# Another order of work in a fused hyena, attention and feed-forward layer: the turn of a batch, the last batch and attention's first tiles

## What is computed

```
x = layernorm(x + hyena(x))        # in-projection to 3 x 256, depthwise conv of 3 taps,
                                   # twice: v = irfft(rfft(v) * rfft(h[n])) * x[n], out-projection
x = layernorm(x + cross_attention(x, ctx))   # 16 heads of 16, 64 context rows per batch
x = layernorm(x + down(silu(gate(x)) * up(x)))  # inner 1024, ternary weights, 8 bit inputs
```

## Time and profile before

| | |
|---|---|
| median of 3 runs | 682.93 us (682.9 to 683.15) |
| profiled execution | 682.95 us, its span 681.0 us |
| TensorE busy | 650.6 us, 96% |
| VectorE busy | 611.0 us, 90% |
| ScalarE busy | 384.5 us, 56% |
| GpSimd busy | 365.1 us, 54% |
| mean granted TensorE clock | 0.998 |

### The profile page before, as it was taken

One profiled execution on the slowest core, in us unless ns is written; L12 is line 12 of the kernel. 1 busy time (PEld: TensorE's weight loads), 2 busy tenths in 40 slices (PEclk: granted clock), 3 DMA queues, 4 the chain that ended last, 5 costly groups with the idle time before them and its releaser, 6 DMA issues. The chain is left out here.

```text
span 681.0 us, 12462 instructions
## 1 busy us (share of the span) xinstructions
PE 650.6 (96%) x4284; PEld 476.8 (70%) x4284; DVE 611.0 (90%) x1241; ACT 384.5 (56%) x761; POOL 365.1 (54%) x506
## 2 busy tenths in 40 slices
PE   9999999999999999999999999888999999999996
PEld 3588765788747887568887677556777775666664
DVE  4899887999999999999999979748999979999997
ACT  3742157131368503475222634569888886888885
POOL 0633424537235753258451381284577769788786
PEclk9999999999999999999999999999999999999999
DMA  8730055230453446443743057552222221010012
GB/s 310 204 63 1 0 125 105 81 62 7 66 107 69 93 155 62 93 93 63 200 100 87 1 185 98 213 174 80 64 80 79 79 79 33 1 34 32 32 63 94
DMA packets 52680, 60.73 MB, mean 89 GB/s; under 512 B 5416, under 2 KB 46376, under 8 KB 52362
## 3 DMA queue, kind: packets, MB, share of 16 engines
q1 hardware_dynamic: 43498, 40.28, 18.3%
q0 software_dynamic: 8256, 18.86, 16.7%
q10 hardware_dynamic: 864, 0.79, 0.4%
HBM read 33.72 MB, written 11.53 MB: 66 GB/s over the span
## 5 line engine op out<-in xcount | busy, mean ns | idle before, releaser
L747 ACT ACTIVATE yb<-banks 128x256 f32<-128x256 f32 x64 | 24.1, 385 | 137.5 <-PE banks L446 92.3
L437 PE MATMUL banks<-inv_m,spec_y 128*128 128x256 f32 x384 | 85.5, 379 | 0.0
L473 PE MATMUL banks<-xt_in,w_in 128*128 128x512 f32 x192 | 84.5, 594 | 0.2
L437 PEld LDWEIGHTS banks<-inv_m,spec_y 128*128 128x128 f32 x384 | 73.0, 190 | 9.9
L389 PE MATMUL banks<-z_cplx,fwd_m 128*128 128x256 f32 x240 | 71.9, 381 | 3.5 <-DVE prod L1172 3.2
L390 PE MATMUL banks<-z_cplx,fwd_m 128*128 128x256 f32 x240 | 71.4, 379 | 0.0
L473 PEld LDWEIGHTS banks<-xt_in,w_in 128*128 128x128 f32 x192 | 36.1, 190 | 43.0 <-issue 40.2
L389 PEld LDWEIGHTS banks<-z_cplx,fwd_m 128*128 128x128 f32 x240 | 44.9, 190 | 11.8 <-issue 5.2
L390 PEld LDWEIGHTS banks<-z_cplx,fwd_m 128*128 128x128 f32 x240 | 45.6, 190 | 6.2
L904 POOL TENSOR_TENSOR spec_y<-prod 128x256 f32<-128x256 f32 x35 | 25.4, 726 | 42.0 <-DVE prod L1172 41.2
L2203 DVE TENSOR_REDUCE peak<-ps_score 128x16 f32<-128x1024 f32 x32 | 38.9, 1215 | 8.7 <-PE ps_score L1668 8.7
(11 more groups left out here) (311 smaller groups left out, 1704.4 us busy)
## 6 DMA issues: line engine op xcount, KB each, us to landing
x_tok<-in_x SPq DMA_DIRECT2D x8, 512.0 KB, 4.3
x_tok<-in_b_out POOLq DMA_DIRECT2D x8, 512.0 KB, 13.9
inv_scratch<-inv_sum SPq DMA_DIRECT2D x16, 256.0 KB, 2.6
xa_t<-inv_scratch SPq DMA_DIRECT2D x16, 256.0 KB, 2.7
v_t<-left POOLq DMA_DIRECT2D x8, 511.5 KB, 5.2
x_t<-left POOLq DMA_DIRECT2D x8, 511.5 KB, 5.6
xt_in<-in_x_t SPq DMA_DIRECT2D x3, 1024.0 KB, 5.9
x_scratch<-x_tok SPq DMA_DIRECT2D x6, 512.0 KB, 4.1
```

The costliest lines, as they stand in the source:

```text
L437: last = mm(bank[:, odd * 2 * P:(odd + 1) * 2 * P], spec_y[:, j + odd, part * D + h * P:part * D + (h + 1) * P], inv_m[:, o:o + 2 * P], st ...
L473: last = mm(proj_pair(b, t)[:, c * 512:(c + 1) * 512], w_in[:, k, TILES[t] * P:(TILES[t] + 1) * P], xt_in[:, k, c * 512:(c + 1) * 512], st ...
```

## The change

Seven edits of order; no arithmetic is added. (1) At the turn of a batch the real pair of `level_one(u + 2, 0)` runs inside `level_two(u + 1, 0)`, and the rotations of the complex pairs run in the next batch, behind the right tap. For that `level_two` keeps its differences in y2 in place of ef. (2) In the last batch `add_residual` is split around `level_two(u, 1)`. (3) There GpSimd makes group 0's factors, four product sums, group 1's factors, and the other sums. (4) ScalarE makes the squares of the last batch's group 0 at the end of `hyena`; `norm_last(0)` no longer waits, and the variance buffer is shared. (5) TensorE's and (6) ScalarE's order of the first six tiles is written out anew, with queries by halves. (7) VectorE's first inverse moves from behind shift 3 to ahead of shift 5.

```diff
@@ hyena, scalar: batch loop's end
             evac_queries(4, IB[0:2])
+            squares(B - 1, (0,))
@@ hyena, gpsimd: batch
                 if last_one:
-                    norm_factors(b - 1)
-                add_products(u + 1)
+                    norm_factors(b - 1, (0,))
+                    add_products(u + 1, 0, 4)
+                    norm_factors(b - 1, (1,))
+                    add_products(u + 1, 4)
+                else:
+                    add_products(u + 1)
@@ hyena, vector: level_two
                 dve.wait_ge(vec_seq, seq.now())
-                signal(tt(ef[:, 0, :], tmp[:, 1, 0:Q], tmp[:, 1, Q:2 * Q], ALU.subtract))
-                signal(tt(ef[:, 1, :], tmp[:, 1, 0:Q], tmp[:, 1, Q:2 * Q], ALU.add))
+                if between is not None:
+                    between()
+                signal(tt(y2[:, 0:Q], tmp[:, 1, 0:Q], tmp[:, 1, Q:2 * Q], ALU.subtract))
+                signal(tt(y2[:, Q:2 * Q], tmp[:, 1, 0:Q], tmp[:, 1, Q:2 * Q], ALU.add))
@@ hyena, vector: batch
                     if not last_one:
                         right_tap(b + 1, T_LEAD)
+                    dve.wait_ge(vec_seq, seq.now())
+                    rotations(in_prod)
                     level_two(u, 0, tmp=past_xq, at=in_prod, u_real=u)
                     level_one(u, 1)
                     dve.wait_ge(vec_seq, seq.now())
                     rotations()
+                    if last_one:
+                        add_residual(b - 1, (0,))
...
                     level_two(u, 1, x0_t[:, 1, :], x0_t[:, 1, :], past_xq, u_real=u)
                     if last_one:
-                        add_residual(b - 1)
+                        add_residual(b - 1, (1,))
...
-                    level_two(u + 1, 0, tmp=past_xq, at=in_prod, u_real=u + 2)
-                    level_one(u + 2, 0, in_prod)
-                    dve.wait_ge(vec_seq, seq.now())
-                    rotations(in_prod)
+                    level_two(u + 1, 0, tmp=past_xq, at=in_prod, u_real=u + 2,
+                              between=lambda: level_one(u + 2, 0, in_prod, complexes=False))
+                    level_one(u + 2, 0, in_prod, real=False)
                     dve.wait_ge(*convolved(b, T_X1 + 1))
                     level_two(u + 1, 1, gate1[:, 1, :], v_t[:, 1, :], past_xq, u_real=u + 2)
@@ attention, tensor (query_half is one of the two bank halves of queries)
             turn_x(Q_EARLY)
-            queries(Q_EARLY)
-            for j in range(TILES_ALL):
+            query_half(Q_EARLY, 0)
+            scores(1)
+            query_half(Q_EARLY, 1)
+            turn_prob(0)
+            turn_x(Q_EARLY + 1)
+            scores(2)
+            turn_prob(1)
+            query_half(Q_EARLY + 1, 0)
+            scores(3)
+            query_half(Q_EARLY + 1, 1)
+            turn_prob(2)
+            turn_x(Q_EARLY + 2)
+            scores(4)
+            turn_prob(3)
+            query_half(Q_EARLY + 2, 0)
+            scores(5)
+            query_half(Q_EARLY + 2, 1)
+            sums(0)
+            scores(6)
+            turn_prob(4)
+            values(0)
+            sums(1)
+            values(1)
+            turn_prob(5)
+            for j in range(6, TILES_ALL):
...
@@ attention, scalar
+            squares_last(0, 2)
             evac_x(Q_EARLY)
-            squares_last(0)
-            for j in range(TILES_ALL):
+            squares_last(2, CH)
+            exponentials(0)
+            act.wait_ge(v_ready, 2 * B)
+            evac_q(Q_EARLY)
+            evac_prob(0)
+            exponentials(1)
+            evac_x(Q_EARLY + 1)
+            evac_prob(1)
+            exponentials(2)
+            evac_q(Q_EARLY + 1)
+            exponentials(3)
+            evac_prob(2)
+            evac_x(Q_EARLY + 2)
+            evac_prob(3)
+            exponentials(4)
+            evac_q(Q_EARLY + 2)
+            weight_sum(0, 0)
+            evac_prob(4)
+            evac_context(0)
+            for j in range(5, TILES_ALL):
...
@@ attention, gpsimd: norm_last
-                pool.wait_ge(l_squared, CH * (g + 1))
+                if g:
+                    pool.wait_ge(l_squared, CH)
@@ attention, vector
+                if j == 5:
+                    invert(0)
                 shift(j)
...
-                if j % 2 and 3 <= j < TILES_ALL - 1:
+                if j % 2 and 5 <= j < TILES_ALL - 1:
                     invert((j - 3) // 2)
```

More of the change, by code:

```diff
@@ L134, in now, with hyena @@
         return self.k
-def hyena(nc, d, x1_dram, fwd_m, w_in, ident, xt_in, x1_even, left, x_toks, row_sum, ld_kv):
+def hyena(nc, d, x1_dram, fwd_m, w_in, ident, xt_in, x1_even, left, x_toks, row_sum, row_var, ld_kv):
     with ExitStack() as ctx:
@@ L763, in row_sums, with squares @@
                     fn(yc[:, 1, :], x_toks[:, g, t, :], ACT.Copy, accum_out=row_sum[:, g, t:t + 1]).then_inc(act_seq, 1)
-            def squares(b):
+            def squares(b, groups=range(GROUPS)):
                 act.wait_ge(first_level, 8 * min(2 * b + 3, 2 * B))
@@ L770, in squares @@
                     act.wait_ge(act_seq, GROUPS * G_OUT * (b + 1) + 1)
-                for g in range(GROUPS):
+                for g in groups:
                     for t in range(G_OUT):
@@ L896, in add_left, with add_products @@
                     .then_inc(conv_done[slot(b, t)], 16)
-            def add_products(u, first=False, prod=prod):
-                for j in range(BANKS - 1):
+            def add_products(u, j0=0, j1=BANKS - 1, first=False, prod=prod):
+                for j in range(j0, j1):
                     pool.wait_ge(prod_done, 8 * u + j + 1)
@@ L951, in add_residual, with norm_factors @@
                     .then_inc(resid_added, 16)
-            def norm_factors(b):
+            def norm_factors(b, groups=range(GROUPS)):
                 ts, tt = nc.gpsimd.tensor_scalar, nc.gpsimd.tensor_tensor
-                for g in range(GROUPS):
+                for g in groups:
                     i = GROUPS * b + g
@@ L1193, in rotations, with level_one @@
                         signal(stt(im, y, -TAN_8, x, ALU.mult, ALU.add))
-            def level_one(u, h, at=None, rotated=False):
+            def level_one(u, h, at=None, rotated=False, real=True, complexes=True):
                 i = 2 * u + h
@@ L1203, in level_one @@
                 split_c = lambda n: yc[:, n, :].rearrange("p (c n) -> p c n", c=2)
-                dve.wait_ge(i_evac, 4 * i + 1)
-                signal(tt(ef[:, 0, :], IB[I_0][:, 0:Q], yb[:, I_0, :], ALU.add))
-                tt(ef[:, 1, :], IB[I_0][:, 0:Q], yb[:, I_0, :], ALU.subtract).then_inc(first_level, 1)
+                if real:
+                    dve.wait_ge(i_evac, 4 * i + 1)
+                    signal(tt(ef[:, 0, :], IB[I_0][:, 0:Q], yb[:, I_0, :], ALU.add))
+                    tt(ef[:, 1, :], IB[I_0][:, 0:Q], yb[:, I_0, :], ALU.subtract).then_inc(first_level, 1)
+                if not complexes:
+                    return
                 for g, bank, factor in ((0, I_2, ROOT_HALF), (1, I_1, COS_8), (2, I_5, COS_8)):
@@ L1214, in level_one, with level_two @@
                         rotations(at, (g,))
-            def level_two(u, h, gate=None, dst=None, tmp=prod, at=None, u_real=None):
+            def level_two(u, h, gate=None, dst=None, tmp=prod, at=None, u_real=None, between=None):
                 i = 2 * u + h
@@ L1275, in quarters_out, with add_residual @@
                 level_two(u, h, gate, dst)
-            def add_residual(b):
-                for g in range(GROUPS):
+            def add_residual(b, groups=range(GROUPS)):
+                for g in groups:
                     dve.wait_ge(biased[g], 16 * (b + 1))
@@ L1464, in attention_loads, with attention_and_feed_forward @@
     return loads
-def attention_and_feed_forward(nc, d, x1_dram, area, small, ident, q_early, x_last, x_last_sum, ld_kv, out):
+def attention_and_feed_forward(nc, d, x1_dram, area, small, ident, q_early, x_last, x_last_sum, l_var, ld_kv, out):
     with ExitStack() as ctx:
@@ L1643, in turn_x, with query_half @@
                     last.then_inc(tr_x, 1)
[L1645 to L1652, removed]
+            def query_half(c, i):
+                if i == 0:
+                    pe.wait_ge(xt_evac, DT * (c - Q_EARLY + 1))
+                t = late_order(c)[i]
+                for k in range(DT):
+                    last = mm(late_banks[t][:, :], wq[:, k, t * P:(t + 1) * P], x_t[:, c % 2, k, :],
+                              start=(k == 0), stop=(k == DT - 1))
+                last.then_inc(q_mm, 1)
             def scores(j):
@@ L1785, in _ @@
                 turn_prob(j)
[L1786 to L1790, removed]
+                if j % 2 == 0:
                     sums(j // 2 - 1)
[L1792 to L1795, removed]
+                    values(j // 2 - 1)
                 if j % 2 and 7 <= j < TILES_ALL - 1:
@@ L1832, in _, with squares_last @@
             fn(table_of[:, 0:1], x_last_sum[:, 0, 0:1], ACT.Exp, scale=0.0)
```

(14 more changed lines are left out.)

9 lines of the change are left out of this document (3 added, 6 removed).

## The result

The changed kernel takes 686.72 us (median of 4 runs, 686.55 to 687.26), the one before 683.04 (4 runs, 682.9 to 683.18): ratio 1.0056, 95% interval 1.0044 to 1.0068. It is slower by 3.7 us. The forecast was 683.4 us, with a range of 680.6 to 685.5. The profiled execution took 686.55, its span is 684.8 us (681.0 before).

A forecast was written before the change was run, and what follows sets the result against it. VectorE was taken to set the pace from batch to batch, with idle time in the last batch and early attention. Terms 0.78 - 1.32 + 1.0 = +0.46 us gave 683.4 us, range 680.6 to 685.5.

The forecast's parts named there:

- Part 1: Turn of a batch, three times: GpSimd's product delays VectorE, 0.26 us each, +0.78 us in all.
- The wait at 263.9: TensorE's 1.11 us wait for VectorE at a batch's turn: would go, its bank coming some 1.1 us sooner.
- the hold: Gated second level: VectorE's first addition held by GpSimd's gating product, 0.26 us a turn, lasting 0.9 instead of 0.69.
- The wait near 290: TensorE's 0.93 us wait for VectorE's right tap: would become about 2 us.
- Part 2: Last batch: earlier GpSimd sums save 1.1 us and additions filling a gap 0.22, -1.32 us in all.
- Part 3: Attention's first tiles: fuller order -0.6 us, GpSimd's holds on VectorE +1.6, together +1.0 us.
- The holds: Attention: GpSimd's scalings and bias addition delay VectorE's paired values and keys; first sum +1.6 us, bounds 0 and 3.4.
- the replay: Attention's new order replayed with the old rows' spacing: without contention the first sum ends as today, order worth -0.6 us.
- the wait of 0.56: Attention, behind the first inverse: VectorE's 0.56 us wait for scores would go.
- B: Attention: stalls of values and keys pass fully to the first sum, 3.4 instead of 1.6; +2.3, 685.2 us; chance 0.19.
- A: VectorE and GpSimd don't hold each other, or keys slip past the bias addition: -1.9, 681.0 us; chance 0.27.
- C: Last batch: VectorE's products 6 and 7 wait for GpSimd sums, the 1.1 is lost: +1.6, 684.5 us; chance 0.06.

The follow-up runs named there:

- the turns alone: The kernel before with only the new turn of a batch, edit (1): 684.57 us, ratio 1.0022.
- attention mended: The kernel before with attention's new order, the first inverse behind shift 5 and the paired keys ahead of GpSimd's bias addition: 679.98 us, ratio 0.9959.
- With the stop filled: The changed kernel with 24 unread identity turns on TensorE between the first sum and scores 6: 686.41 us, ratio 1.0050.
- with the inverse behind shift 5: The changed kernel with only the first inverse moved back behind shift 5 in VectorE's queue: 682.61 us, ratio 0.9994.
- the rows early: The changed kernel with the load of chunk 4's rows issued right behind group 0's reload: 686.61 us, ratio 1.0055.
- all three: The changed kernel with the first inverse behind shift 5, keys ahead of the bias addition and chunk 4's rows loaded early: 679.15 us, ratio 0.9943.
- attention alone: The kernel before with only attention's new order, edits (4) to (7): 686.4 us, ratio 1.0048.

## Why the prediction was wrong

**Part 1, +0.78: right.** 0.77 in the trace of the turns alone, 0.64 at the queries of the changed kernel. The wait at 263.9 is gone and the hold is where it was put. The wait near 290 is not 2 but 0.33 + 1.21, in two places. The Trainium skill, "SBUF — State Buffer", section "Who interferes with whom", says that a VectorE instruction with two SBUF inputs contends with a GpSimd instruction that reads SBUF. The traces agree: the addition took 0.95 us beside GpSimd's product and 0.69 without, and the keys, the pair that no row of the first trace had, took 2.99 us beside the bias addition and 1.02 without.

**Part 2, -1.32: the gain right, the cover wrong.** -1.24 from the queries to the inverse transform. What failed is "From there to the end of the stage TensorE has no gap, so the 1.1 is kept". I followed group 1 to one customer, the bias DMA, and found 3 us of cover. The load of chunk 4's rows stands behind that group's store and reload in SyncE's queue, and it was not in my list. Its cover looked ample: the rows used to land at about 407.5 and are wanted at 415.67, so the 2.06 us of later issue alone would have cost nothing. That the load would take 11.2 us to land in place of 5.0 was in no row, and its cause stays open; issued at 397.20 it took 4.8. Together the two gave back 1.46. Group 1's factors came when I expected them, about 399.

**Part 3, +1.0: the failed step, 2.5 us short.** Measured is +1.93 to the first inverse and +1.60 to the second, and nothing of it comes back behind. The sign of being right that I had named, the second inverse within 1.5 us of its old distance from the barrier, failed with 3.5. The holds were sized nearly right: 1.22 for the keys is shown, and attention mended, which has the keys first, still has its first inverse 0.69 us later behind the barrier than the kernel before; together 1.91, forecast 1.6. The stop was in the replay too: shift 5 until 459.6, and scores 6 behind it, which leaves TensorE idle for 3.4 us from 456.2. What failed is the sentence "The inverse follows at the same time as today; only the wait of 0.56 for scores behind it goes". It gave the steps behind the stop the spacing of rows in which the granted clock was 1.00. They ran in part at 0.50, and the distance of the two inverses became 8.62 in place of 7.02. With the stop filled it is 7.04, so the replay of the order was right and the 1.58 us are the clock, which was in no term of the sum and no rival: I never asked what a stop of TensorE would do to it. The 0.56 did not go either. It comes back before shift 8 (475.57), since ScalarE's copy of tile 4 waits until 466.24 for values 0 and ScalarE works without a gap from there:
```profile
466.24 1.02 ACT L1897 ACTIVATE prob_t<-ps_pt 128x1024 f32<-128x1024 f32 x1 [7.12 <-PE ps_ctx L1716]
```
```profile
475.57 1.23 DVE L2236 TENSOR_REDUCE peak<-ps_score 128x16 f32<-128x1024 f32 x1 [0.56 <-PE ps_score L1680]
```
So part 3 is short by 0.3 (holds), 1.6 (clock) and 0.6 (the wait that stayed), and part 2 by 1.5. By this sum either the clock or the rows alone would have left the time within the range; the two together put it outside. What the replay also missed is no part of the error but the larger lesson: with the inverse behind shift 5 the second inverse follows 3.7 us behind the first, not 7.

**The rivals.** B named keys and values as the slow side and a size of 3.4. The time lies on its side, but not for its reason: TensorE waited 1.16 us before scores 3, not over 2, and the keys' 1.2 is a third of the loss. A did not happen: the keys took 2.99 us, not 1.02. The sign of C did appear: product 6 waited 1.54 us for a GpSimd sum, above the mark of 1 us:
```profile
400.57 0.69 DVE L1175 TENSOR_TENSOR prod<-banks,spec_h 128x512 f32<-128x512 f32 x1 [1.54 <-POOL spec_y L905]
```
But TensorE ran on without a gap into the inverse transform (399.80), so the gain was not lost there, and the mark was not a good one.

## What to carry to other kernels

When an instruction that waits for another engine is moved ahead of one that is ready, the price is the wait of whoever needs the second one: replay both queues, write down the idle time of the engine that sets the pace, and replay the other order too before choosing. When a transfer gets late, list every transfer behind it in its issuing queue, and don't take its landing time from the old trace: here 5.0 us became 11.2. And before a gain is called lost, look at the clock behind the nearest stop of TensorE: two real gains, of 1.2 and 1.55 us, were invisible in the times until the stop was filled.

## What the runs showed of the hardware

Whether the granted clock falls depends on the instant as well as on the stop. In the same stop of 3.42 us it fell about 1.0 us before scores 6 with the rows early, while TensorE still stood, and about 0.4 us behind their start in the changed kernel (worked out from the clock of the 2 us stretches); from barrier to second inverse the first cost 1.14 us more. Long stops are not needed. With stops of at most 1.58 us in the stretch it stayed at 1.00 in the kernel before and fell to 0.50 from 469 to 472 in the kernel with the turns alone, which then was 1.6 us further behind. In the execution of all three that was profiled it fell at about 202 us, behind stops of 0.33 and 1.21, and 1.1 us were lost in the middle of the convolution; the other five executions of that kernel have a clock of 0.998. The kernel before has a clock of 0.996 in 3 of its 66 executions on the three chips, and these took 685.0 to 685.5 us. The Trainium skill, "TensorE: Matmul & The Clock Gate", section "Part 1: The HAM clock gate", says that the gate follows how busy TensorE has been recently and that the same kernel meets it at different phases. These runs agree: with the stop filled the clock stayed at 1.00, and six executions of attention alone have 0.993 to 0.999. What sets the phase, no run here shows.

The start of an execution varies by up to 1 us (5.83 to 6.87 for the same product). That was not expected either; it is as large as most single terms of this sum, so terms were read as distances within a trace.
